# A two-layer decoder on one core: head similarity by a square root for the last batches, early clears, and new instruction orders

## The reference, cut to what matters

```python
x = ln(x + L0_attn(x))    # gated causal convolution (Mamba-like), no attention
x = ln(x + L0_xattn(x, ctx))   # cross attention, 16 heads of 64, 77 keys
x = ln(x + L0_ffn(x))     # shared expert + 8 experts, 2 chosen per token
x = ln(x + L1_attn(x))    # self attention with rotary positions, 16 heads of 16
x = ln(x + L1_xattn(x, ctx))
x = ln(x + L1_ffn(x, g_info))  # attention over all 2048 tokens in batches, with a mask
```

```python
q, k, v = (x @ W_qkv).reshape(B, N, 3, H, D)
q_n  = q / norm(q);  qg_n = q_g / norm(q_g)
sim  = (qg_n * q_n).sum(-1).mean(-1)          # mean over the 16 heads
sim  = (sim - sim.min()) / (sim.max() - sim.min())   # over ALL tokens
pos  = sim > 0.9
out  = attention whose keys are restricted to pos, or to not pos
```

## Time and profile before

| | us |
|---|---|
| median of three runs | 1488.07 |
| the profiled execution's own time | 1488.75 |
| span of its trace | 1486.6 |
| PE busy | 1306.3 (88%) |
| DVE busy | 972.3 (65%) |
| ACT busy | 651.4 (44%) |
| POOL busy | 424.1 (29%) |

### The profile page before, as it was taken

The page is one execution under the profiler, slowest core; times in us unless marked ns, Lnnn a source line. Parts: engine busy times, 40 slices in busy tenths (PEclk is TensorE's granted clock), DMA queues, the critical chain, the costliest instruction groups (busy, mean ns, idle before and its releaser), DMA issues.

```text
span 1486.6 us, 27795 instructions
## 1 busy us (share of the span) xinstructions
PE 1306.3 (88%) x11854; PEld 1088.3 (73%) x11854; DVE 972.3 (65%) x1785; ACT 651.4 (44%) x806; POOL 424.1 (29%) x405
## 2 busy tenths in 40 slices
PE   6989999999999999997678979989979957888776
PEld 6788889888878889997457757758858745546453
DVE  3766777768776446777556766876766646566673
ACT  6544555546542434663234334345334431432413
POOL 5141030210421754665203325325305330000000
PEclk9989999999999999999699999999999966978988
DMA  8371200111051223883100110110101120010000
GB/s 294 121 258 35 49 18 19 49 35 33 18 203 52 87 78 130 275 281 120 44 2 18 32 37 22 50 36 22 35 1 43 50 79 22 23 58 16 2 16 15
DMA packets 46138, 103.33 MB, mean 70 GB/s; under 512 B 4336, under 2 KB 26480, under 8 KB 45120
## 3 DMA queue, kind: packets, MB, share of 16 engines
q1 hardware_dynamic: 42944, 93.18, 18.9%
q0 software_dynamic: 3072, 8.39, 1.8%
HBM read 64.79 MB, written 36.77 MB: 68 GB/s over the span
## 4 chain that ended last, share of the span: by engine, by line
PE 69%; DVE 19%; ACT 5%; POOL 3%; issue 2%; DMA 1%; SPq 0%; POOLq 0%; DVEq 0%; ACTq 0%
PE ps L881 9%; DVE sm L1959 8%; PE ps L167 7%; PE ps L168 7%; PE ps L169 7%; PE ps L1345 4%; PE ps L182 4%; PE ps L1078 4%; PE ps L187 4%; PE ps L183 4%; PE ps L1094 3%; PE ps L1351 3%; PE ps L1326 3%; DVE m L1948 2%; ACT m L1814 2%
## 5 line engine op out<-in xcount | busy, mean ns | idle before, releaser
L1557 ACT ACTIVATE m<-ps 128x1024 f32<-128x1024 f32 (+5 forms) x184 | 151.8, 840 | 296.2 <-PE ps L169 105.3
L1959 DVE TENSOR_REDUCE sm<-ps 128x8 f32<-128x2048 f32 (+1 forms) x128 | 195.3, 1536 | 73.9 <-PE ps L1326 53.0
L1557 ACT ACTIVATE r<-ps 128x512 fp32r<-128x512 f32 (+1 forms) x159 | 101.1, 639 | 203.0 <-PE ps L881 106.9
L2645 POOL TENSOR_SCALAR sm<-sm 128x2 f32<-128x2 f32 x40 | 8.8, 221 | 633.4 <-DVE sm L1977 633.4
L1948 DVE TENSOR_TENSOR r<-ps,r 128x512 fp32r<-128x512 f32 (+1 forms) x159 | 116.5, 740 | 108.1 <-ACT r L1557 107.5
L1814 ACT ACTIVATE m<-ps 128x2048 f32<-128x2048 f32 x64 | 119.5, 1878 | 105.6 <-PE ps L1345 105.5
L881 PE MATMUL ps<-cst,m 128*77 128x128 f32 (+2 forms) x1024 | 140.4, 281 | 18.5 <-DVE m L1948 8.5
L881 PEld LDWEIGHTS ps<-cst,m 128*77 128x77 f32 (+2 forms) x1024 | 117.3, 148 | 43.5 <-issue 14.7
L1326 PE MATMUL ps<-m 32*128 32x256 f32 x1024 | 95.6, 505 | 27.3 <-DVE sm L1959 23.3
L2672 POOL TENSOR_TENSOR m<-m,sm 128x616 f32<-128x616 f32 x64 | 77.7, 1225 | 124.0 <-DVE sm L2133 124.0
L1326 PEld LDWEIGHTS ps<-m 32*128 32x128 f32 x1024 | 61.4, 241 | 55.6 <-DVE sm L1959 40.0
(11 more groups left out here) (324 smaller groups left out, 3618.4 us busy)
## 6 DMA issues: line engine op xcount, KB each, us to landing
raw<-wu_dram SPq DMA_DIRECT2D x20, 768.0 KB, 5.5
keep_dram<-kept SPq DMA_DIRECT2D x8, 768.0 KB, 3.3
m<-keep_dram SPq DMA_DIRECT2D x8, 768.0 KB, 4.3
xs_dram<-gsq SPq DMA_DIRECT2D x2, 2944.0 KB, 16.4
ys_dram<-m SPq DMA_DIRECT2D x23, 256.0 KB, 2.8
room<-wu_dram SPq DMA_DIRECT2D x7, 768.0 KB, 5.1
rt<-xs_dram SPq DMA_DIRECT2D x16, 256.0 KB, 3.7
w1raw<-w_dram SPq DMA_DIRECT2D x1, 3840.0 KB, 12.0
```

The costliest lines, as they stand in the source:

```text
L1557: return act.activation(o, i, ACT.Copy)
L1959: return dve.tensor_reduce(o, i, AX.X, op, **kw)
```

## The change

Five edits:

- `likeness` of batches 0 to 5 is issued in the next cross attention of its stream, behind the sums of its rounds 2 and 3, and no longer right behind `dq`.
- For batches 6 and 7 the power on POOL is gone. ACT takes the square root of `qq` (step `root`, between `c1` and `c2`), DVE takes the reciprocal (`inv`) and one Newton step (`n1` to `n4`).
- `qg` moves behind `gq`, and the small tiles `qq`, `dq`, `inv`, `t` move from `sm` into columns 6784 to 6911 of `m`.
- POOL's `blank` for batches 0 and 1 is issued right after `last_moe`, ahead of the wait for the stores and of the clear of `w1f`.
- All tables of `FIRST` and `SECOND` have new numbers. `LAST` is as it was.

```diff
 FIRST = {
     "PE": [
-        6, 6, 6, 6, 6, 6, 19, 19, 19, 19, 21, 21, 21, 21, 23, 23, 23, 27, 28, 29, 32, ...
+        5, 6, 6, 6, 6, 6, 21, 21, 21, 21, 21, 21, 21, 21, 23, 23, 23, 27, 27, 27, 27, ...
...
+        def norms_of(st):
+            return [k2(st.m[3][:, a:a + 32]) for a in range(6784, 6912, 32)]
...
+                if b + 2 >= B:
+                    act.wait_ge(*st.q_dve.at(b, "gq"))
+                    act.activation(norms_of(st)[2], norms_of(st)[0], ACT.Sqrt).then_inc(sig.up(b, "root"), 1)
+                    yield
                 act.wait_ge(*pe_.at(b, "qkv"))
                 copy(qkv[:, :, 512:768], k2(bank(st, 3))).then_inc(sig.up(b, "c2"), 1)
...
                 for u in range(2, 4):
                     yield from sums(u)
+                    yield
+                if L and b >= 2:
+                    yield from likeness(st, b - 2)
                     yield
...
             def likeness(st, b):
-                sig, qq, dq = st.q_dve, k2(st.sm[:, 32:64]), k2(st.sm[:, 64:96])
+                sig, (qq, dq, inv, t) = st.q_dve, norms_of(st)
                 dve.wait_ge(*sig.at(b, "dq"))
-                dve.wait_ge(*st.q_pool.at(b, "pow"))
-                tt(dq, dq, qq, ALU.mult).then_inc(sig.up(b, "sc"), 1)
+                if b + 2 < B:
+                    dve.wait_ge(*st.q_pool.at(b, "pow"))
+                    inv = qq
+                else:
+                    dve.wait_ge(*st.q_act.at(b, "root"))
+                    dve.reciprocal(inv, inv).then_inc(sig.up(b, "inv"), 1)
+                    yield
+                    dve.wait_ge(*sig.at(b, "inv"))
+                    tt(t, inv, qq, ALU.mult).then_inc(sig.up(b, "n1"), 1)
+                    dve.wait_ge(*sig.at(b, "n1"))
+                    tt(t, t, inv, ALU.mult).then_inc(sig.up(b, "n2"), 1)
+                    yield
+                    dve.wait_ge(*sig.at(b, "n2"))
+                    ts(t, t, -0.5, 1.5, ALU.mult, ALU.add).then_inc(sig.up(b, "n3"), 1)
+                    dve.wait_ge(*sig.at(b, "n3"))
+                    tt(inv, inv, t, ALU.mult).then_inc(sig.up(b, "n4"), 1)
+                    yield
+                    dve.wait_ge(*sig.at(b, "n4"))
+                tt(dq, dq, inv, ALU.mult).then_inc(sig.up(b, "sc"), 1)
...
-                tt(qg, qv, gvec.unsqueeze(1).to_broadcast([P, 2, 256]), ALU.mult).then_inc(sig.up(b, "qg"), 1)
-                yield
...
                 tt(qq, qq, gg.unsqueeze(1).to_broadcast([P, 2, 16]), ALU.mult).then_inc(sig.up(b, "gq"), 1)
                 yield
+                tt(qg, qv, gvec.unsqueeze(1).to_broadcast([P, 2, 256]), ALU.mult).then_inc(sig.up(b, "qg"), 1)
+                yield
...
-                yield from likeness(st, b)
-                yield
+                if b + 2 >= B:
+                    yield from likeness(st, b)
+                    yield
...
+            last_moe(pool)
+            for st in streams:
+                for _ in blank(st, st.i):
+                    pass
+            for i in range(2):
+                pool.wait_ge(d_ys[i], 16 * ((NT + 1 - i) // 2))
+            pool.wait_ge(d_w1f, 16)
+            pool.memset(w1f[:, 0:2464], 0.0).then_inc(k1_zero.up("zero"), 1)
+            for st in streams:
+                pool.memset(st.sm[:, 128:384], 0.0).then_inc(st.nm_pool.up("zero"), 1)
...
             def fq(st, b):
...
-                pool.wait_ge(*st.q_dve.at(b, "gq"))
-                pool.tensor_tensor(qq, qq, k2(mhalf), ALU.pow).then_inc(sig.up(b, "pow"), 1)
-                yield
+                if b + 2 < B:
+                    pool.wait_ge(*st.q_dve.at(b, "gq"))
+                    pool.tensor_tensor(qq, qq, k2(mhalf), ALU.pow).then_inc(sig.up(b, "pow"), 1)
+                    yield
```

More of the change, by code:

```diff
@@ L43 @@
     "PE": [
[6 rows of a table removed]
-    "ACT": [
[5 rows of a table removed]
-    "DVE": [
[7 rows of a table removed]
[6 rows of a table added]
+    "ACT": [
[5 rows of a table added]
+    "DVE": [
[7 rows of a table added]
     "POOL": [
-        1, 4, 5, 8, 9, 11, 13, 13, 13, 13, 13, 13, 15, 16, 16, 16, 16, 18, 21, 22, 25, 26, 28, 30, 30, 30, 30, 30, 30, 32, 33, 33, 33, 33, 35, 38, 39, 42, 43, 45,
-        47, 47, 47, 47, 47, 47, 49, 50, 50, 50, 50, 52, 55, 56, 59, 60, 62, 64, 64, 64, 64, 64, 64, 66, 67, 67, 67, 67],
+        3, 3, 3, 12, 12, 12, 12, 12, 12, 12, 12, 12, 15, 15, 15, 20, 20, 20, 20, 20, 26, 26, 26, 26, 29, 29, 29, 29, 29, 32, 32, 32, 41, 41, 41, 41, 41, 46, 46, 46,
+        46, 46, 46, 46, 46, 46, 49, 49, 49, 54, 54, 54, 54, 54, 58, 58, 58, 58, 63, 63, 63, 63, 63, 66, 66, 66],
 }
@@ L69 @@
     "PE": [
[7 rows of a table removed]
[7 rows of a table added]
         282, 282],
     "ACT": [
[5 rows of a table removed]
-    "DVE": [
[7 rows of a table removed]
[5 rows of a table added]
+    "DVE": [
[7 rows of a table added]
     "POOL": [
[3 rows of a table removed]
+        0, 0, 0, 0, 13, 13, 13, 18, 18, 18, 18, 19, 19, 20, 21, 21, 21, 21, 26, 26, 26, 26, 26, 26, 26, 26, 35, 35, 35, 40, 40, 40, 40, 41, 41, 42, 42, 42, 44, 44,
+        44, 47, 49, 49, 49, 49, 49, 49, 49, 59, 59, 59, 64, 64, 64, 64, 64, 64, 64, 64, 64, 66, 66, 67, 70, 70, 70, 70, 70, 70, 77, 77, 77, 77, 77, 78, 79, 82, 82, 82,
+        82, 82, 85, 85, 85, 85, 85],
 }
@@ L483, in program @@
             st.q_pe = Signal(sem(f"q_pe{i}"), steps(["xT", "qk0", "qk1", "qkv"], bs))
-            st.q_act = Signal(sem(f"q_act{i}"), steps(["xT", "c0", "c1", "c2"], bs))
-            st.q_dve = Signal(sem(f"q_dve{i}"), steps(["xT", "sq", "qg", "rq", "gq", "dq", "sc", "sim"], bs))
-            st.q_pool = Signal(sem(f"q_pool{i}"), steps(["bias", "pow"], bs))
+            st.q_act = Signal(sem(f"q_act{i}"), [(b, s) for b in bs for s in ["xT", "c0", "c1", *(["root"] if b + 2 >= B else []), "c2"]])
+            st.q_dve = Signal(sem(f"q_dve{i}"), [(b, s) for b in bs for s in ["xT", "sq", "rq", "gq", "qg", "dq", *(["inv", "n1", "n2", "n3", "n4"] if b + 2 >= B else []), "sc", "sim"]])
+            st.q_pool = Signal(sem(f"q_pool{i}"), [(b, s) for b in bs for s in ["bias", *(["pow"] if b + 2 < B else [])]])
             st.nm_pool = Signal(sem(f"nm_pool{i}"), [("zero",)])
@@ L2476, in fq @@
                 qkv, sq, qg = k2(st.kept[:, :]), k2(m[:, a:a + 512]), k2(m[:, a + 512:a + 1024])
-                qq, dq = k2(st.sm[:, 32:64]), k2(st.sm[:, 64:96])
+                qq, dq = norms_of(st)[0:2]
                 turned_x(st, b, xT_of(st, 3), act_, sig, bank(st, 2))
@@ L2767, in _ @@
                     pass
-            last_moe(pool)
-            for i in range(2):
-                pool.wait_ge(d_ys[i], 16 * ((NT + 1 - i) // 2))
-            pool.wait_ge(d_w1f, 16)
-            pool.memset(w1f[:, 0:2464], 0.0).then_inc(k1_zero.up("zero"), 1)
-            for st in streams:
-                pool.memset(st.sm[:, 128:384], 0.0).then_inc(st.nm_pool.up("zero"), 1)
             def blank(st, b):
@@ L2789, in blank @@
                 z.then_inc(sig.up(b, "z"), 1)
+            last_moe(pool)
[8 more added lines that the diff above has]
+                pool.memset(st.sm[:, 128:384], 0.0).then_inc(st.nm_pool.up("zero"), 1)
             def a1_front(st, b):
-                yield from blank(st, b)
+                if b >= 2:
+                    yield from blank(st, b)
+                else:
+                    yield
                 yield
@@ L2806, in fq @@
                 sig = st.q_pool
-                qq = k2(st.sm[:, 32:64])
+                qq = norms_of(st)[0]
                 pool.wait_ge(*st.x_dve[1].at(b, "ln"))
```

## The result

| | before | after |
|---|---|---|
| median, runs of one chip | 1487.87 us (4) | 1466.38 us (4) |
| ratio | | 0.9854, 95% interval 0.9835 to 0.9873 |
| profiled execution, span | 1488.75, 1486.6 | 1467.53, 1465.7 |

The change makes the kernel 21.5 us faster. The sign held, and the range (1465 to 1487) held by 1.4 us at its lower end; the gain is twice the forecast's 10.7.

The account below looks back on a forecast made before the run. PE's idle time was taken as the bound, with PE 69% of the chain. Terms -2 - 2 - 5 + 0 - 2.4 = -11.4 us took the profiled 1488.75 us to 1477.4, range 1465 to 1487.

Parts of the forecast that it names:

- Layer 0, first pair: Layer 0's head: batch 1's products of y fill PE's hole before batch 0's transpose; -2 us, range 0 to -4.5.
- Layer 0, the rest: Layer 0's later pairs: an earlier transpose covers L173's waits, -3.5 at best; other swaps may open gaps; -2 us taken.
- Head of layer 1: Layer 1's start: earlier blanks shrink PE's 3.44 us hole and keep the clock up; -5 us, between -2.7 and -7.1.
- The middle: Layer 1's middle: moving likeness gives -1 to 0 directly, the new table either sign; 0 us, range -5 to +5.
- The end: Layer 1's end: square root replaces POOL's power, ACT's clear and the store then bound the choice; -2.4 us, -0.4 to -2.5.
- C: Rival, clearly faster: every hole closes, -21 us, 1467.7 us; chance 13%.
- A: Rival, slower: layer 1's new middle order adds 22 us of PE waits, 1499 us; slower from 15.9 us; chance 9%.
- B: Rival, hardly any change: savings at both layers' heads are given back, last store late; -4.1 us, 1484.7 us; chance 18%.
- D: Rival at layer 1's end: square root changes nothing because the stores decide, 1479.4 us; counted within the forecast's 60%.

Follow-up runs that it names:

- e9: Kernel before, with the odd batch's transpose moved between the halves of z in layer 0's second to fourth pair, on PE, ACT and DVE; ratio 0.9986.
- e10: Changed kernel with the move of the odd batch's transpose between the halves of z undone on PE, ACT and DVE; ratio to before 0.9837.
- e7: Kernel before with the square root alone for batches 6 and 7, old tables and late blanks; ratio 0.9976.
- e8: The changed kernel itself, run again without any edit; ratio to before 0.9857.
- e1: Kernel before with the changed table FIRST (layer 0's order) alone; ratio 0.9897.
- e6: Kernel before with the changed FIRST, early blanks and the square root, but old SECOND and old place of likeness; ratio 0.9828.
- e4: Changed kernel with POOL's power again for batches 6 and 7 in place of the square root; ratio to before 0.9867.
- e2: Changed kernel with the table FIRST (layer 0's order) of before; ratio to before 0.9933.
- e3: Kernel before, with the odd batch's transpose moved between the halves of z in layer 0's second to fourth pair, on PE and ACT only; ratio 1.0008.
- e12: Kernel before with the square root for batches 6 and 7 and the blanks ahead, all orders old; ratio 0.9905.

## Why the prediction was wrong

By its own steps:

1. *Layer 0, first pair, -2:* right within the spread. At the first scores the eight profiles with the new FIRST are 1.1 to 3.5 us ahead of the profile of before, 2.5 on the mean; the six with the old one, that profile among them, 0 to 2.1, on the mean 1.2. That is -1.3 for the order. The slow clock behind the hole was foreseen; the hole itself stayed at 5.19 us and not 3.7.
2. *Layer 0, the rest, -2 (at best -6):* **the step that failed.** It measured -9.6 between the first scores and L1186 in the two profiles, beyond its best of -6. The one wait that the step priced, L173's, is worth 2.0 to 2.5 (e9, e10), so that term was near its value. The step called the other edits swaps that "can open a gap of the same size", gave them both signs alike and so the value 0. The runs show in its place that they closed 5.2 us of the waits of L191 and L881 (5.4 idle us in all), which stood in the same list as L173's 4.2, with 5.4 and 3.8. The lower bound, half of the idle time less what the ends hold, rested on no row; 20.5 us of idle time allowed more.
3. *Head of layer 1, -5:* right as an effect of the blanks in the old order (5.3 ± 0.9, some 2 us of it idle time and the rest less busy time, as PE was slower for less of it). In the changed kernel it measured -7.4, of which 2.4 us is work moved behind the first scores, so -5.0 is closed idle time. Not foreseen was that the new SECOND closes the same hole, so that there the two don't add, and the clock did not come up to 0.9 (0.80). That the sum is right is in part luck.
4. *The middle, 0:* +3.2 in the traces, inside the ±5; 2.3 of it is the work that the head no longer does, and 0.8 new idle time.
5. *The end, -2.4:* right in size (2.5 in e7; 3.5 with the new order), wrong in what takes over: DVE's own chain, not ACT's clear or a store. The exponential's table is loaded again, as foreseen, in a gap of ACT: from 1193.61 for 1.28 us, with 3.71 us of idle time before its next user.
6. *What the sum left out:* the experts took 245.9 us before and 244.0 after, with 6.3 us of PE's idle time in both. All fourteen profiles lie between 243.2 and 245.9, and that of before is the longest. The masked attention took 1.3 us more, less than it differs between two executions of one kernel (2.8 us, e8). I put both down to the execution; for the experts this is not shown.

The rivals: C had named a closing of the holes at 1467.7 and gave it 13%; it is the nearest in time, but by luck, since it had the first pair at -4.5 and the steady part at -6. A fell, with 0.8 us of new idle time in the middle against the 15.9 that it needed. B fell (e1, e6: leads are kept), and so did D (e4, e7).

## What to carry to other kernels

Price a new order by the waits it could close, all of them, from the list of waits with its sums, and not by the one whose cure the diff shows plainly. To give the unread part of an order the value zero is a guess like any other; here it was worth more than the part that was read. Before adding two edits that fill the same hole, ask what each leaves for the other; and where an execution's time hangs on the granted clock, compare the starts of fixed instructions, and beside them times at equal mean clock, remembering that such a correction also hides what a kernel gains by its clock. A stretch that gets shorter may only have handed work to the next: count the products in both.

## What the runs showed of the hardware

In the old order of layer 0 the clock fell in five of six profiles at two short waits in a row, without any long one. The two waits in e7 and windows of PE around them:

```profile
266.75 0.41 PE L191 MATMUL ps<-ctxAh,kw2h 128*128 128x308 f32 x1 [1.17 <-DVE stage L2055]
...
268.58 1.11 PE L884 MATMUL ps<-cst,xres 128*128 128x128 f32 x4 [0.87 <-DVE xres L1960]
```

```profile
262.00:268.00 6.00, 4.54 (x35) 1.00 0.40 104
268.00:271.50 3.50, 2.92 (x13) 0.55 0.00 0
271.50:290.00 18.50, 17.55 (x142) 0.99 0.24 64
```

The middle row is nearly all at the 1.2 GHz level. In the profile of before the same place, with waits of 1.18 and 0.87 us, stayed at 1.00,

```profile
268.00:272.00 4.00, 3.09 (x23) 1.00 0.00 0
```

so the two waits alone do not decide it, and what else does is open. This place fell in e2, e3, e7 and e12, a later one of the kind (362 to 367 us) in e2, e3, e7 and e9, and neither in any of the eight profiles with the new FIRST, where the longest wait of L191 is 0.9 us. That the closed waits spared the clock too would explain why runs of the old order lose up to 2.4 us more in layer 0 than the profile of before did, on which the forecast was made.
